# Gated blocks with their rows 8 KB apart in DRAM, and rows of norms and biases repeated by the host for each partition

## What is computed

```
x1 = x + layernorm(x + relu(x W1[lang] + b1) W2[lang] + b2) * gamma0[lang] + beta0[lang]
ctx     = decaying sum of x1 over time (one decay)
gated   = x1 * sigmoid([x1, ctx] Wg + bg)
m[d]    = 0.5 + sigmoid(gelu(x1 Wn1 + bn1) Wn2 + bn2)          d = 0..7
trace_d = decaying sum over time of gated * m[d], with decay d
temporal = sum over d of blend[d] * trace_d
out = x1 + layernorm((gelu(x1 Wsoma + bsoma) * sigmoid(temporal Wtemp + btemp)) Wout) * gamma1 + beta1
```

## Time and profile before

| | |
|---|---|
| median of 3 runs | 1368.03 us (1366.42 to 1370.3) |
| profiled execution | 1361.66 us, its span 1359.8 us |
| granted TensorE clock, mean | 0.996 |
| busy share of the span | TensorE matmul 97%, its weight load 73%, VectorE 76%, ScalarE 38%, GpSimd 28% |
| DMA | 186.25 MB, mean 137 GB/s; the SyncE queue 42.4% and the ScalarE queue 3.7% of 16 engines |

### The profile page before, as it was taken

The page is one execution under the profiler, slowest core; times in us unless marked ns, Lnnn a source line. Parts: engine busy times, 40 slices in busy tenths (PEclk is TensorE's granted clock), DMA queues, the critical chain, the costliest instruction groups (busy, mean ns, idle before and its releaser), DMA issues.

```text
span 1359.8 us, 19735 instructions
## 1 busy us (share of the span) xinstructions
PE 1312.5 (97%) x7908; PEld 991.4 (73%) x7908; DVE 1028.8 (76%) x1526; ACT 521.1 (38%) x822; POOL 373.9 (28%) x294
## 2 busy tenths in 40 slices
PE   4889999999999999999999999999999999999997
PEld 2657778677786867768677686777868777786766
DVE  7988677887778777677786768777787786778575
ACT  3425243443524424243343433425244252434422
POOL 4405142051411404133131422304123041421102
PEclk9999999999999999999999999999999999999999
DMA  8382542907247180561706526074451825426060
GB/s 268 130 223 88 156 154 78 240 32 207 103 116 202 70 240 31 149 200 62 218 32 175 174 78 202 32 224 124 117 169 65 232 78 156 154 79 169 36 182 32
DMA packets 91486, 186.25 MB, mean 137 GB/s; under 512 B 9858, under 2 KB 14594, under 8 KB 87298
## 3 DMA queue, kind: packets, MB, share of 16 engines
q1 hardware_dynamic: 82178, 168.20, 42.4%
q10 hardware_dynamic: 9216, 16.78, 3.7%
HBM read 134.61 MB, written 50.33 MB: 136 GB/s over the span
## 4 chain that ended last, share of the span: by engine, by line
PE 36%; DVE 23%; DMA 16%; issue 13%; ACT 6%; SPq 2%; POOL 2%; DVEq 0%; POOLq 0%
PE ring L984 26%; DVE U L863 11%; DMA grep<-g_blocks 8%; DMA g_blocks<-g_f 7%; PE ring L977 4%; SPq L355 2%; DVE x L793 2%; DVE stats L798 2%; ACT U L523 2%; DVE g_f L872 2%; PE Tp L1158 1%; PE Tp L1169 1%; DMA x<-g_blocks 1%; POOL rows L441 1%; PE ring L1183 1%
## 5 line engine op out<-in xcount | busy, mean ns | idle before, releaser
L863 DVE TENSOR_TENSOR U<-grep,w_qs 128x1024 f32<-128x1024 f32 x192 | 227.3, 1219 | 56.9 <-issue 36.7
L412 POOL TENSOR_TENSOR x<-grep,b_row 128x512 f32<-128x512 f32 x64 | 80.5, 1289 | 547.5 <-DMA grep<-in_x 547.5
L1158 PE MATMUL Tp<-U,Arep 128*32 128x256 f32 x2048 | 133.6, 385 | 13.9 <-DVE U L863 13.2
L533 ACT ACTIVATE g_f<-g_f 128x512 f32<-128x512 f32 x64 | 40.4, 632 | 259.3 <-DVE g_f L868 259.1
L425 POOL TENSOR_TENSOR grep<-grep,beta_row 128x512 f32<-128x512 f32 x64 | 82.8, 1327 | 116.7 <-DMA grep<-x_tiles 116.6
L1158 PEld LDWEIGHTS Tp<-U,Arep 128*32 128x32 f32 x2048 | 54.1, 109 | 79.3 <-DVE U L863 39.6
L868 DVE TENSOR_TENSOR g_f<-ring,bg_row 128x512 f32<-128x512 f32 x64 | 44.1, 689 | 85.2 <-PE ring L984 85.2
L984 PE MATMUL ring<-seq_hi,Wtemp_hi 128*128 128x512 f32 x256 | 106.7, 417 | 0.1
L984 PE MATMUL ring<-x1T_hi,Wsoma_hi 128*128 128x512 f32 x256 | 103.2, 403 | 0.0
L984 PE MATMUL ring<-Wg_hi,x1T_hi 128*128 128x512 f32 x256 | 103.2, 403 | 0.0
L984 PE MATMUL ring<-Wout_hi,g_r 128*128 128x512 f32 x256 | 99.8, 390 | 1.1 <-DVE soma_r L720 1.0
(11 more groups left out here) (173 smaller groups left out, 2878.8 us busy)
## 6 DMA issues: line engine op xcount, KB each, us to landing
grep<-g_blocks SPq DMA_DIRECT2D x192, 256.0 KB, 4.5
grep<-in_xc SPq DMA_DIRECT2D x16, 1024.0 KB, 10.8
grep<-in_x SPq DMA_DIRECT2D x16, 1024.0 KB, 9.0
x_tiles<-x SPq DMA_DIRECT2D x16, 1024.0 KB, 9.0
g_blocks<-g_f ACTq DMA_DIRECT2D x64, 256.0 KB, 3.8
x<-g_blocks SPq DMA_DIRECT2D x64, 256.0 KB, 5.3
grep<-x_tiles SPq DMA_DIRECT2D x16, 1024.0 KB, 4.8
out<-U SPq DMA_DIRECT2D x64, 256.0 KB, 2.0
```

The source lines that it names most:

```text
L412: nc.gpsimd.tensor_tensor(new[:, b, :], x_t[:, b, :], b2_row[:, :], ALU.add).then_inc(xb2_ready, 1)
L533: nc.scalar.activation(g[:, b, :], g[:, b, :], ACT.Sigmoid).then_inc(sig_ready, 1)
L863: V_.tensor_tensor(U[:, (n + 2) % 4, :, :], spans_of(k, b)[:, :, at], w_qs[:, hh, at].unsqueeze(1).to_broadcast([P, NI, HC]), ALU.mult).th ...
L1158: last = nc.tensor.matmul(Tp[b % 2][i * L:(i + 1) * L, at], Arep[:, b * NI + i, hh, :], U[:, (n + 2) % 4, i, :], start=(hh == 0 and c == 0 ...
```

## The change

The first edit gives each row of a gated block four times its length in DRAM and uses the first quarter: rows of 2 KB now begin 8 KB apart, and a block covers 1 MB. The second edit has the host write `b2`, `gamma0`, `beta0`, `bg`, `gamma1` and `beta1` out once for each of 128 partitions, so that the loads read 128 different rows of 2 KB in a piece of 256 KB. The SBUF side of every DMA, its size and its place in the order stay.

```
-        g_dram = nc.dram_tensor("g_blocks", [NB, P, C], F, kind="Internal").ap()
+        g_dram = nc.dram_tensor("g_blocks", [NB, P, 4 * C], F, kind="Internal").ap()[:, :, 0:C]
...
-                sp.dma_start(b2_row[:, :], b2[bass.ds(one, 1)].to_broadcast([P, C])).then_inc(ld_b2, 16)
+                sp.dma_start(b2_row[:, :], b2[bass.ds(one, 1)].rearrange("a p m -> p (a m)")).then_inc(ld_b2, 16)
...
-                    sp.dma_start(row[:, :], src[bass.ds(one, 1)].to_broadcast([P, C])).then_inc(ld_norm, 16)
+                    sp.dma_start(row[:, :], src[bass.ds(one, 1)].rearrange("a p m -> p (a m)")).then_inc(ld_norm, 16)
...
-                    sp.dma_start(row[:, :], src.to_broadcast([P, C])).then_inc(ld_rows, 16)
+                    sp.dma_start(row[:, :], src).then_inc(ld_rows, 16)
...
+    each = lambda v: c(np.broadcast_to(np.asarray(v)[..., None, :], np.asarray(v).shape[:-1] + (P, C)))
-        "b2": c(L0_cond_b2), "g0": c(L0_cond_gamma), "be0": c(L0_cond_beta),
+        "b2": each(L0_cond_b2), "g0": each(L0_cond_gamma), "be0": each(L0_cond_beta),
-        "bg": np.asarray(L1_cond_bg).reshape(1, C), "g1": np.asarray(L1_cond_gamma).reshape(1, C),
-        "be1": np.asarray(L1_cond_beta).reshape(1, C), "cols": c(cols), "taus": c(tau_table),
+        "bg": each(L1_cond_bg), "g1": each(L1_cond_gamma), "be1": each(L1_cond_beta), "cols": c(cols), "taus": c(tau_table),
```

More of the change, by code:

```diff
@@ L1293 @@
     cols = np.concatenate([np.asarray(L1_cond_bn1)[:, None], by_chunk(L1_cond_bsoma), by_chunk(L1_cond_btemp)], axis=1)
+    each = lambda v: c(np.broadcast_to(np.asarray(v)[..., None, :], np.asarray(v).shape[:-1] + (P, C)))
     arrays = {
         "x": c(xs), "xc": c(xs.transpose(0, 2, 1)), "ids": np.asarray(itok_B_0_8).reshape(1, BATCHES),
-        "w1": c(L0_cond_W1), "w2": c(L0_cond_W2), "b1": c(L0_cond_b1), "b2": c(L0_cond_b2),
-        "g0": c(L0_cond_gamma), "be0": c(L0_cond_beta),
+        "w1": c(L0_cond_W1), "w2": c(L0_cond_W2), "b1": c(L0_cond_b1), "b2": each(L0_cond_b2),
+        "g0": each(L0_cond_gamma), "be0": each(L0_cond_beta),
         "wg": c(np.asarray(L1_cond_Wg).T), "wn1": c(np.asarray(L1_cond_Wn1).T), "wsoma": c(np.asarray(L1_cond_Wsoma).T),
         "wtemp": c(np.asarray(L1_cond_Wtemp).T), "wout": c(np.asarray(L1_cond_Wout).T), "wn2": c(np.asarray(cond_256).T),
-        "bg": np.asarray(L1_cond_bg).reshape(1, C), "g1": np.asarray(L1_cond_gamma).reshape(1, C),
-        "be1": np.asarray(L1_cond_beta).reshape(1, C), "cols": c(cols), "taus": c(tau_table),
+        "bg": each(L1_cond_bg), "g1": each(L1_cond_gamma), "be1": each(L1_cond_beta), "cols": c(cols), "taus": c(tau_table),
         "bn2": np.asarray(condB_bn2).reshape(1, D),
```

## The result

The changed kernel takes 1427.45 us (median of 4 runs, 1425.84 to 1431.1) against 1367.22 us (median of 4): a ratio of 1.0441, 95% interval 1.0414 to 1.0468. The profiled execution took 1427.39 us with a span of 1425.6. The prediction, 1367 us and 1355 to 1376, was wrong; its rival (b) is what happened, in kind.

The account below looks back on a forecast made before the run. TensorE was taken to bound the kernel, with 13 us lost to a DMA round trip. Edit 1 at 0, edit 2 at 0 and 1 us of gain made 1360.7 us profiled, 1367 us as median; range 1355 to 1376.

Parts of the forecast that it names:

- rival (b): Block stores and reads: gaps touch four times as much DRAM; block 2 1.0 us longer costs 16 us; chance 0.14.
- What bounds the kernel: TensorE is the path; L1158 waits 13.2 us for VectorE, which waits for block reads; lateness beyond cover is paid 16 times.
- Edit 2: Loads of a language's rows: 118 GB/s goes, input lands earlier, nobody waits for it; worth 0, within 1 us each way.
- the sum: Whole kernel: 0 for each edit, 1 us of gain allowed for shorter queues; 1360.7 us profiled, 1367 us as median.
- Edit 1: Block stores and reads with rows 8 KB apart: reads stay at 229 to 257 GB/s, so worth 0 us.
- The limit on the side of SBUF: Block reads, writing 32 partitions each, are held at 229 to 257 GB/s by SBUF's side under any DRAM layout.

Follow-up runs that it names:

- e14: The kernel before with only the second edit, and a block's four reads issued for quarters 0, 2, 1, 3: 1357.34 us, ratio 0.9934.
- e1: The kernel before with only the first edit, rows of gated blocks 8 KB apart: 1425.0 us, ratio 1.0423.
- e10: The kernel before, its block reads taking another buffer with rows 8 KB apart, stores staying at 2 KB: 1426.92 us, ratio 1.0456.
- e3: The kernel before with its four blocks interleaved in 1 MB, rows of one block 8 KB apart without gaps: 1431.28 us, ratio 1.0461.
- e13: DMAs alone, no kernel: wide 1 MB DMAs, then four narrow reads of four blocks or one; at 8 KB 7.3 to 7.4 against 7.5 to 8.6 us.

## Why the prediction was wrong, point by point

*What bounds the kernel* held. TensorE is the path, L1158 waits for VectorE and VectorE for the block's reads, "issue" is a DMA wait (it rose from 36.7 to 61.1 us with the reads), and what a block is late beyond its cover is paid in each of 16 tiles.

*Edit 2* held in all its steps: 118 GB/s became 379; in slot 6 the transposed input landed 9.1 us after its issue instead of 12.0, as forecast; nobody waited for it; alone it gave 0.9999. GpSimd's L412 started 0.3 us before the end of slot 6 instead of 3.4 us behind it, within the 3 to 4 us earlier that were forecast. Edit 2 gave nothing beside the earlier blocks of `e14` either. The 1 us of gain that the sum allowed for it was not seen.

*Edit 1* is the step that failed, where the prediction says "I therefore expect the reads to stay at 229 to 257 GB/s, limited on the side of SBUF, and take 0 us for the edit." The reads fell to 178 to 189 GB/s, and the term put at 0 measured 58 us (1425.0 against 1366.91 us, `e1`). The price was taken from the nearest row, the input's 400 GB/s. But that load has its rows 2 KB apart; it says that DRAM can give more than the reads take at 2 KB, and nothing of 8 KB. A block's four reads are a burst of 1 MB that starts from rest, four times in each tile, all four from the same rows, and VectorE waits for its end. At 8 KB its first read took 0.8 us longer (3.1 to 3.9) and the four 1.2 us (6.7 to 7.9). `e10` shows that the distance in the buffer that is read does this by itself.

*The limit on the side of SBUF* was half right. Reads into 128 partitions were faster than into 32 (4.7 to 5.4 against 6.2 to 6.6 us), and the order of the quarters, which changes only where the reads write, helps before; so the reads before were held at least in part by where they write. That doesn't protect them from the DRAM layout, though the prediction held that it would: their rate fell with nothing changed on the side of SBUF. At 8 KB they run below the rate that this side allowed before, and the order had no effect that the runs can tell.

The rule of the page "DMA: Bandwidth & Descriptors" of the Trainium skill, section "Latency and other measured facts", on large powers of two, which I had set aside as 8 KB is far below its distances, pointed the right way: 4 and 8 KB cost 2.2% and 4.2% here, 6 and 10 KB 0.8% and 0.7%. Its advice to pad by a few KiB agrees with these runs; its half rate does not, as no read here took twice the time.

*Rival (b)* had the direction and the path, and too small a price and chance. Its signs came: a rate below 200 GB/s, VectorE's waits for `grep<-g_blocks` over 30 us (57.9), and an odd slot above 82 us (86.59). Its reason, that four times as much DRAM is touched, did not hold: `e3` touches no more than before and lost as much. It reckoned 16 us for each microsecond of one block, block 2. But all four blocks are late, and they stand in one row: the store of block 1 is 1.6 us longer, most of it because of the slower reads beside it (1.3 us in `e10`), its reads start later, and so on to block 3, whose reads are complete 14.5 us after its store's issue instead of 11.8. VectorE waited 4.2 us more in a slot (67 / 16) and TensorE paid 3.8. For block 2 alone, whose four reads take 0.9 us longer (7.3 to 8.2), (b)'s rule would have given 15 us.

**What stays open.** Why these distances collide in DRAM, and why reading one block four times makes it worse, was not tried further. How much depends on where a buffer lies is open too: the narrow read of one block at 8 KB took 6.7 to 6.8 us in one program and 7.3 to 8.6 in two others, though three kernels with differently declared buffers (`e1`, `e3`, `e10`) lost nearly the same, 4.2 to 4.6%. Why a store beside reads took 5.6 us in the kernel and 4.3 alone isn't settled. That the limit on the 32 partitions is one of ports was not tried.

## What to carry to other kernels

A rate read at one layout prices no other layout. Here a row at 2 KB was taken to price 8 KB, and a program of some DMAs alone would have shown the difference, though not its full size. Price a DMA that someone waits for by its time from issue to landing, in the pattern and the repetition in which the kernel issues it. Where the rows of a tile go to DRAM and come back, keep them without gaps, and if they must be apart, try a distance that is no power of two (10 KB cost 0.7% here and 8 KB 4.2%). When a round trip is on the path, the order in which its parts are issued is worth a try before its addresses: quarters 0, 2, 1, 3 gave 0.6% for nothing with blocks without gaps.

## What the runs showed of the hardware

- Four reads of 256 KB into 32 partitions each, rows of 2 KB (`e13`): the first landed after 3.0 us with rows 2 KB apart, after 3.9 us at 8 KB. The further three took 3.4 us in both from four different blocks, and 3.6 to 4.8 us at 8 KB when one block was read four times.
- A kernel with 64 such bursts on its path was slower by 2.2% at 4 KB, 0.8% at 6 KB, 4.2% at 8 KB and 0.7% at 10 KB.
- A store of 256 KB from 128 partitions took 2.0 us by itself at 2, 4, 6, 10 and 16 KB, and 2.3 to 2.4 at 8 KB in two programs of three.
- One row of 2 KB read 512 times took 7.8 us, 512 reads of 128 different rows 4.7 to 5.4 us. In the kernel such loads ran at 118 GB/s, and nobody was waiting.
